# The causal mask of a head loop, added by a product on TensorE instead of by VectorE

## What is computed

```python
causal_mask = jnp.tril(jnp.ones((SEG, SEG), bool))
def step(carry, seg):
    mem, z = carry
    qq, kk, vv = seg
    sigma_q = jax.nn.elu(qq) + 1.0
    scores = jnp.einsum('bhsk,bhtk->bhst', qq, kk) / scale
    scores = jnp.where(causal_mask, scores, -jnp.inf)
    att_dot = jax.nn.softmax(scores, axis=-1) @ vv
    att_mem = sigma_q @ mem / (sigma_q @ z)
...
    att = beta * att_mem + (1.0 - beta) * att_dot
    out = att.reshape(Bsz, SEG, H * DV) @ Wo
```

## Time and profile before

| | us |
|---|---|
| median of three runs | 561.98 (561.61 to 562.02) |
| the profiled execution | 559.13 |
| its span, first to last instruction | 557.4 |
| busy: TensorE, its loads | 498.6, 417.9 |
| busy: VectorE | 355.7 |
| busy: ScalarE | 320.2 |
| busy: GpSimd | 144.1 |
| mean granted TensorE clock | 0.954 of full |

### The profile page before, as it was taken

How to read it: one execution, slowest core, us unless ns; L and a number is a source line. 1 busy time by engine, 2 the same in 40 slices (tenths; PEclk the granted TensorE clock), 3 DMA queues, 4 the chain that set the end, 5 groups by cost and what they waited for, 6 DMA issues and landing times. The chain is left out here.

```text
span 557.4 us, 11832 instructions
## 1 busy us (share of the span) xinstructions
PE 498.6 (89%) x4164; PEld 417.9 (75%) x4165; DVE 355.7 (64%) x782; ACT 320.2 (57%) x762; POOL 144.1 (26%) x141
## 2 busy tenths in 40 slices
PE   8989999999999999999899799996737999999960
PEld 3768888887898888888689667774624888888850
DVE  5367777776654777776666377777372666666654
ACT  4377777778626777777672389996203444444430
POOL 5110000003100000000000439998011455555530
PEclk9989999999999999999999899999559999999995
DMA  9421111111010111120000024443213355454527
GB/s 266 160 57 44 55 55 55 56 58 58 19 39 20 56 47 53 55 56 20 0 2 1 1 82 148 145 135 101 68 41 113 119 169 168 144 157 152 169 76 226
DMA packets 24001, 48.05 MB, mean 86 GB/s; under 512 B 2960, under 2 KB 11168, under 8 KB 23968
## 3 DMA queue, kind: packets, MB, share of 16 engines
q1 hardware_dynamic: 21120, 41.17, 24.2%
q0 software_dynamic: 2240, 6.04, 3.1%
q10 hardware_dynamic: 608, 0.39, 0.3%
HBM read 42.48 MB, written 5.11 MB: 85 GB/s over the span
## 5 line engine op out<-in xcount | busy, mean ns | idle before, releaser
L666 PE MATMUL psum<-a_xt_hi,a_qk_hi 128*128 128x512 f32 x128 | 54.6, 426 | 0.0
L1409 POOL DMA_INDIRECT picks_dram<-x_wout,e_pick_row x23 | 38.8, 1685 | 51.8 <-DVE x_wout L1572 51.8
L666 PE MATMUL psum<-a_xt_hi,a_qk_lo 128*128 128x512 f32 x128 | 50.6, 395 | 0.0
L666 PE MATMUL psum<-a_xt_lo,a_qk_hi 128*128 128x512 f32 x128 | 50.5, 394 | 0.0
L987 ACT ACTIVATE x_probs<-psum,x_neg_max 128x128 f32<-128x128 f32 x128 | 45.9, 406 | 6.7 <-DVE x_neg_max L1044 6.7
L1450 ACT ACTIVATE e_inner_hi<-psum 128x512 fp32r<-128x512 f32 x23 | 13.8, 599 | 57.7 <-PE psum L1632 57.7
L578 DVE COPY a_weights_t<-psum 64x256 f32<-64x256 f32 x32 | 13.7, 428 | 49.4 <-PE psum L782 49.4
L916 POOL MEMSET x_mask<- 128x512 bf16 x1 | 0.5, 525 | 167.5 <-POOLq L250 167.5
L444 ACT ACTIVATE a_probs<-a_shifted 128x256 f32<-128x256 f32 x32 | 13.4, 419 | 50.1 <-DVE a_shifted L544 50.1
L796 PE MATMUL psum<-a_weights_t,a_v 64*128 64x64 f32 x256 | 34.9, 275 | 8.0 <-issue 4.1
L1623 PE MATMUL psum<-expert_w_hi,e_x_hi 128*128 x92 | 38.3, 416 | 2.2 <-DVE e_x_lo L1550 2.2
(11 more groups left out here) (238 smaller groups left out, 1513.5 us busy)
## 6 DMA issues: line engine op xcount, KB each, us to landing
x_k_t<-in_expert_wo SPq DMA_DIRECT2D x23, 512.0 KB, 3.5
a_qk_raw<-in_wqk SPq DMA_DIRECT2D x32, 256.0 KB, 2.6
x_xn_t<-in_expert_w SPq DMA_DIRECT2D x16, 512.0 KB, 3.8
a_wv_raw<-in_wv SPq DMA_DIRECT2D x17, 256.0 KB, 2.7
x_sb<-in_x SPq DMA_DIRECT2D x2, 512.0 KB, 5.0
x_k_t<-in_wo SPq DMA_DIRECT2D x1, 1024.0 KB, 10.4
x_v<-in_wo SPq DMA_DIRECT2D x1, 1024.0 KB, 12.9
xn_dram<-xn SPq DMA_DIRECT2D x1, 1024.0 KB, 4.4
```

Of the source, the lines that this page charges most:

```text
L666: last = pe.matmul(out, pick_l(left[a], k), pick_r(right[b], k), start=start and n == 0, stop=n == 3 * KD - 1, skip_group_check=not start)
L1409: pool.indirect_dma_start(out=picks_dram, out_offset=bass.IndirectOffsetOnAxis(ap=pick_row[:, tile:tile + 1], axis=0), in_=y_rows[:, slot, ...
```

## The change

In front of every head's soft scores TensorE multiplies the bf16 permutation with the bf16 mask into bank 2 (256 columns, as the start of an accumulation), and the eight score products now accumulate on it (`start=False`). VectorE's add is gone; its maximum and its subtraction read bank 2. The single mask product before the loop, VectorE's copy of it, the tile `mask_f` and two semaphores go.

```diff
@@ attention_phase: tiles and semaphores
-    mask_f = sb("a_mask_f", [P, HB * SEG], F32)
-    mask_mixed, masked_ready = sem("mask_mixed"), sem("masked_ready")
@@ VectorE, before the loop
-            dve.wait_ge(mask_mixed, 1)
-            dve.tensor_copy(mask_f[:, :], c.bank[3][:, 0:HB * SEG])
@@ VectorE, step
                 dve.wait_ge(soft_done, s.n + 1)
-                dve.tensor_tensor(shifted[:, :, :, :].rearrange("p j g t -> p (j g t)"), c.bank[2][:, 0:HB * SEG], mask_f[:, :],
-                                  ALU.add).then_inc(masked_ready, 1)
-                dve.wait_ge(masked_ready, s.n + 1)
-                dve.tensor_reduce(row_max[:, :, :], shifted[:, :, :, :], AX.X, ALU.max).then_inc(max_ready, 1)
+                dve.tensor_reduce(row_max[:, :, :], soft_ps, AX.X, ALU.max).then_inc(max_ready, 1)
                 dve.wait_ge(max_ready, s.n + 1)
-                dve.tensor_tensor(shifted[:, :, :, :], shifted[:, :, :, :], row_max[:, :, :].unsqueeze(3).to_broadcast([P, HP, 2, SEG]),
+                dve.tensor_tensor(shifted[:, :, :, :], soft_ps, row_max[:, :, :].unsqueeze(3).to_broadcast([P, HP, 2, SEG]),
                                   ALU.subtract).then_inc(shifted_ready, 1)
@@ TensorE, soft_scores
                 pe.wait_ge(qk_ready, n * 2 + 2)
 
+                pe.matmul(c.bank[2][:, 0:HB * SEG], mixed_b[:, :], mask[:, :, :], start=True, stop=False,
+                          skip_group_check=True)
                 for b in range(HB):
                     for seg in (b % 2, 1 - b % 2):
                         at = slice(seg * SEG, (seg + 1) * SEG)
                         last = pe.matmul(soft_ps[queries_at(b, seg), b // 2, 1 - seg, :], q_sb[:, b, at], k_sb[:, b, at],
-                                         start=True, stop=True, skip_group_check=True)
+                                         start=False, stop=True, skip_group_check=True)
@@ TensorE, before the loop
             pe.wait_ge(consts_ready, 6)
-            pe.matmul(c.bank[3][:, 0:HB * SEG], mixed_b[:, :], mask[:, :, :], start=True, stop=True).then_inc(mask_mixed, 1)
             transpose_x(0)
```

## The result

| | before | changed |
|---|---|---|
| median of 19 runs each | 561.5 us (558.27 to 568.57) | 559.19 us (554.74 to 567.14) |
| profiled execution | 559.13 us, span 557.4 | 557.68 us, span 555.9 |
| mean granted clock in it | 0.954 | 0.964 |

The ratio is 0.9942 (95%: 0.9914 to 0.997), so the change takes 0.58% off, about 3.3 us, where 1.27 us were forecast. A second session gave 557.73 us (12 runs) against 561.12 us (23), ratio 0.9954 (0.992 to 0.9987), about 2.6 us. The forecast's 0.23% lies inside the second interval and just outside the first. The ratios are taken over undisturbed executions alone, the medians of the table over all, which is why these lie only 2.3 us apart.

The account below looks back on a forecast made before the run. TensorE was taken as nearly always busy, with line 796 waiting on ScalarE's copy. Terms -0.46 + 0.11 - 0.46 - 0.46 = -1.27 us moved the median 561.98 to 560.7 us; range 558.9 to 563.1.

Parts of the forecast that it names:

- Item 1: VectorE's add goes in 32 heads: -0.46 us each in heads 0, 13 and 15, nothing elsewhere.
- Item 2: Mask product before each head's soft scores fits TensorE's 0.22 us hole: 0 booked in regular heads, bounds 0 to +2.4 us.
- Rival A: Mask product paid in full, 0.11 us in each of 27 heads: 563.7 us; chance 0.10.
- the +2.4 us end of the range: Item 2's upper bound: an insertion costing 0.31 us less the 0.22 hole, 0.09 us in 27 heads.
- Items 3 to 5: Head 0's mask product, +0.11 us; product and copy removed at the start, 0; VectorE's longer wait for scores, 0.
- Rival C: Another wait stands right behind the chain in heads 0, 13 and 15, so nothing moves: 561.9 us; chance 0.13.
- rival B: Clock drop from 34.52 to 37.93 us stays away: -1.7 us more, 559.0 us; chance 0.22.
- D: Clock drops fall otherwise on the shifted work, one added or longer: +1.7 on the sum, 562.4 us; chance 0.05.

Follow-up runs that it names:

- The fillers: Kernel before plus nine discarded bf16 products of 256 columns in TensorE's wait of head 0: 558.55 us, ratio 0.9921; in the changed kernel 557.57 us.
- the kernel with two products more: Kernel before with two discarded bf16 products of 64 columns in front of every head's soft scores: 567.37 us, a single run.

## Why the prediction was half right

**Item 1, the softmax chain: right.** The add's 0.46 us is gone, reading PSUM costs nothing more, and it counts where the chain has no slack: 0.42 in head 0 (in the medians of five profiles 0.40, 30.45 to 30.05; forecast 0.35, with the product's 0.11 in it), 0.46 in heads 13 and 15. The copy there starts 0.62 us behind the last transpose, forecast 0.66. It counts nowhere else.

**Item 2, the product in regular heads: right at 0.** The change of array shape is paid once, not twice (0.20 us from the mask product to the soft scores, as from the transpose before). Mask_first, the run with the product ahead of the transposes, shows the price that is hidden, 0.12 us. The Trainium skill, "TensorE: Matmul & The Clock Gate", section "Back-to-back issue gap", gives a gap of N/2.4 + 2.5 ns for a product by itself, so 109 ns here, an estimate; the trace agrees within 0.01 us. What the page does not say is whether anyone waits for them. Rival A is out, and so is the +2.4 us end of the range.

**Items 3 to 5: nothing speaks against them.** Head 0's product stands in its place; its 0.11 us cannot be told apart from the spread of single profiles.

**Rival C is out** by the three heads' columns. The sum was -1.27 us, measured -1.32, -1.02 and -1.39 in paired profiles and -1.7 +- 0.4 at equal clock over the second session.

**The step that failed is the clock.** The sum put it at nothing, and of rival B I wrote that "the stretch stays a thin one, so I hold it less likely than not". B gave 0.22; the drop was gone in three of five profiles of the changed kernel, in none of five of before. B's price, 1.7 us, was near the measured 1.5 (10.24 against 8.70 in head 0 to 1). As an estimate from these counts the share near 34 us is 3/5 x 1.5 = 0.9 us. With the 1.0 to 1.4 us of the heads that makes 1.9 to 2.3 us, where the ratios give 3.3 and 2.6 us, in intervals that begin at 1.7 and 0.7. What may be left belongs to the other drops, whose length and place differ from execution to execution (30.7 us from 389.5 in the first of before, 23.9 us from 392.75 in the first of the changed kernel); no run shows what of it is the change's. The reason I gave failed too: how thin the stretch is does not settle it alone, since the same stretch had the drop or not by where one could begin. So the sum needed a term for the drop, its price times how often it comes in either kernel. That 559.19 us lies on B's 559.0 is partly luck: B is one drop in one place, and the median of before had itself moved from 561.98 to 561.5. D, which looked for a loss there, had the sign wrong.

**What stays open.** Whether, and how far, the change makes the drop near 34 us rarer: five of five against two of five is too few to tell. The fillers show that more work there keeps it away, and the range of places with a drop was narrower with the shorter chain; but all five profiles without it and without fillers are ones where the place lay outside the range seen with it, and two of them have the old chain. And whether less time is spent in the other drops, where the kernels are the same.

## What to carry to other kernels

Before booking a product on the busiest engine, look for a wait inside its period that it can sit behind: the same product cost 0 us behind the transposes and 0.12 us in front of them. Read heads or iterations that have no slack one by one; the 1.3 us lay in three of 32. Where a profile shows the clock drop in a thin stretch, one profile tells neither its chance nor its place: the stretch deserves a term of its own in the sum, the later drops of each profile show where it could have begun, and pairs with the same drops must be compared. Set every kernel beside the old one of its own session: the old one alone moved by 1 us between sessions.

## What the runs showed that was not expected

**Two paces of the same code.** The regular period is 7.09 or 7.13 us for the whole loop of an execution, at granted clock 1.00 throughout, in either kernel. The difference, 0.034 us, lies in the twelve products of q and k; the rest of the head repeats within 0.01 us. It comes to some 1 us over the loop, as much as the change's own arithmetic. Its cause is open.

**The low clock varies by execution.** 43 to 57 us of a 557 us span on average, by the kernels of the table, with a standard deviation of 3 to 7 us: at 0.32 us each, some 2 us of spread between executions of one kernel.

**A long drop at the loop's end.** Three of the 20 profiles, of three kernels, have a drop of 20.48 us that starts between 274.5 and 276.8 us; they are also the three with the longest spans (562.6, 565.6 and 565.6 us). In the third profile of before, the stretch ahead of it, the end of that stretch, and nearly all of the drop; then the drop of the kernel with two products more:

```profile
250.00:276.70 26.70, 24.95 (x254) 20.86 (x253) 18.00 (x45) 18.26 (x37) 0.00 (x0) 1.00 0.04 10
...
273.35:276.76 3.41, 2.24 (x32) 1.71 (x27) 2.37 (x6) 1.73 (x5) 0.00 (x0) 1.00 0.00 0
...
276.76:297.20 20.44, 20.44 (x66) 14.15 (x65) 7.54 (x10) 10.82 (x16) 0.00 (x0) 0.50 0.00 1
```

```profile
274.50:294.98 20.48, 20.48 (x66) 14.24 (x66) 7.69 (x11) 10.76 (x16) 0.00 (x0) 0.50 0.00 0
```

TensorE was busy for 24.95 of the 26.70 us ahead, but most of the idleness stands at their end, where it was busy for 2.24 of 3.41 us and waited 1.17 us in one piece before head 30's weight-value products. The Trainium skill, in the same page's section "HAM oscillation — how this bites in real kernels", lays the falls of the clock to TensorE's idle gaps; in kind this drop's start and the one near 34 us agree with that, though no gap ahead of either is longer than 1.2 us. Its length is another matter: TensorE was busy in all of the 20.44 us and the clock stayed at 0.50, while the drop near 34 us ended after 3.41 or 6.83 us of a busy TensorE. Why is open.
